# Twelve weight loads of the first expert loop: issued behind the loop's own tile count, one unit at a time

## What is computed

```python
def _L0_ffn_ref(x, gate_w, W1, b1, W2, b2, sW1, sb1, sW2, sb2):
    logits = x_flat @ gate_w.T                       # 8 experts
    probs = softmax(logits)
    top_w, sel = top_k(probs, 2)                     # two experts for each token
    top_w = top_w / sum(top_w)
    h = gelu(einsum('th,ehf->tef', x_flat, W1) + b1) # H = 256, F = 1024
    y = einsum('tef,efh->teh', h, W2) + b2
    out = einsum('teh,te->th', y, combine)
    out = out + gelu(x_flat @ sW1 + sb1) @ sW2 + sb2 # one shared expert
x = x + tanh(g_xattn[0]) * L0_xattn(layernorm(x), ctx)
x = x + tanh(g_ffn[0])   * L0_ffn(layernorm(x))
x = x + tanh(g_xattn[1]) * L1_xattn(ctx, layernorm(x))
x = x + tanh(g_ffn[1])   * L1_ffn(layernorm(x))
```

## Time and profile before

| what | us |
|---|---|
| median of 3 runs | 801.63 |
| lowest and highest | 799.29, 803.27 |
| the profiled execution | 800.92 |
| its span in the trace | 799.1 |
| PE busy | 686.3 (86%) |
| DVE busy | 512.9 (64%) |
| ACT busy | 462.8 (58%) |
| POOL busy | 311.2 (39%) |
| mean granted TensorE clock | 0.915 of 2.4 GHz |

### The profile page before, as it was taken

One profiled execution on the slowest core, in us unless ns is written; L12 is line 12 of the kernel. 1 busy time (PEld: TensorE's weight loads), 2 busy tenths in 40 slices (PEclk: granted clock), 3 DMA queues, 4 the chain that ended last, 5 costly groups with the idle time before them and its releaser, 6 DMA issues.

```text
span 799.1 us, 22223 instructions
## 1 busy us (share of the span) xinstructions
PE 686.3 (86%) x7654; PEld 604.3 (76%) x7655; DVE 512.9 (64%) x1286; ACT 462.8 (58%) x1124; POOL 311.2 (39%) x227
## 2 busy tenths in 40 slices
PE   4787899988958999999999918771799999999993
PEld 3454566767858999999989917661689999999993
DVE  4569758796855975777755445948398555555551
ACT  2346668856527976777755605440497656556561
POOL 1100124335541554555544422340256545455442
PEclk9878889999988999999999977955799999999997
DMA  8950100013429433688753359528223232232331
GB/s 264 296 185 27 53 1 1 35 46 130 136 81 369 81 52 65 140 242 228 221 164 49 38 151 408 206 97 228 65 47 48 47 51 46 46 53 42 49 47 21
DMA packets 63235, 91.07 MB, mean 114 GB/s; under 512 B 6203, under 2 KB 48965, under 8 KB 62422
## 3 DMA queue, kind: packets, MB, share of 16 engines
q1 hardware_dynamic: 48118, 69.69, 25.9%
q0 software_dynamic: 15072, 20.84, 16.6%
HBM read 63.73 MB, written 26.79 MB: 113 GB/s over the span
## 4 chain that ended last, share of the span: by engine, by line
PE 63%; DVE 15%; DMA 9%; issue 5%; ACT 5%; SPq 1%; POOL 1%; POOLq 0%; DVEq 0%; ACTq 0%
PE bank L1123 8%; PE bank L1125 7%; PE bank L1124 7%; PE bank L1136 6%; PE bank L1137 6%; PE bank L1138 6%; DMA x_arena<-token_rows,gather_now 4%; PE bank L1106 2%; DMA x_sum<-x_arena,add_now 2%; DMA out<-x_arena,add_now 2%; DVE weights L1568 2%; DVE ln_stats L1890 2%; PE bank L849 2%; PE bank L1019 1%; PE bank L1021 1%
## 5 line engine op out<-in xcount | busy, mean ns | idle before, releaser
L1419 ACT ACTIVATE work<-bank,b_cols 128x128 f32<-128x128 f32 x624 | 177.5, 371 | 172.1 <-PE bank L1125 154.8
L1123 PE MATMUL bank<-x_arena,weights 128*128 128x128 f16 x1248 | 220.2, 222 | 0.3 <-DVE x_arena L1801 0.3
L1124 PE MATMUL bank<-x_arena,weights 128*128 128x128 f16 x1248 | 220.1, 221 | 0.0
L1125 PE MATMUL bank<-x_arena,weights 128*128 128x128 f16 x1248 | 219.8, 221 | 0.0
L1816 DVE TENSOR_TENSOR work<-work 128x512 f16<-128x512 f32 x156 | 101.2, 690 | 140.6 <-ACT work L1427 118.4
L1137 PE MATMUL bank<-weights,work 128*128 x624 | 170.1, 273 | 0.0
L1136 PE MATMUL bank<-weights,work 128*128 x624 | 170.1, 273 | 0.0
L1138 PE MATMUL bank<-weights,work 128*128 x624 | 170.1, 273 | 0.0
L715 POOL DMA_INDIRECT x_arena<-token_rows,gather_now x80 | 100.2, 1252 | 78.3 <-issue 53.8
L1124 PEld LDWEIGHTS bank<-x_arena,weights 128*128 x1248 | 124.2, 100 | 0.0
L1123 PEld LDWEIGHTS bank<-x_arena,weights 128*128 x1248 | 122.8, 98 | 1.1 <-issue 0.5
(11 more groups left out here) (219 smaller groups left out, 1263.5 us busy)
## 6 DMA issues: line engine op xcount, KB each, us to landing
weights<-in_L_ffn_W SPq DMA_DIRECT2D x76, 256.0 KB, 7.7
raw<-in_L_ffn_W SPq DMA_DIRECT2D x44, 256.0 KB
split_dram<-row_arena SPq DMA_DIRECT2D x12, 512.0 KB
weights<-split_dram SPq DMA_DIRECT2D x3, 2048.0 KB, 15.4
token_rows<-row_arena SPq DMA_DIRECT2D x2, 2072.0 KB, 11.3
x_arena<-in_x SPq DMA_DIRECT2D x4, 512.0 KB, 6.6
weights<-in_L_ffn_sW SPq DMA_DIRECT2D x8, 256.0 KB, 7.3
x_sum<-x_arena SPq DMA_DIRECT2D x4, 512.0 KB, 2.9
```

The costliest lines, as they stand in the source:

```text
L1123: nc.tensor.matmul(o, w1_at[f][c][0].block(), hi, start=c == 0, stop=False)
L1124: nc.tensor.matmul(o, w1_at[f][c][0].block(), lo, start=False, stop=False)
L1125: m = nc.tensor.matmul(o, w1_at[f][c][1].block(), hi, start=False, stop=c == DC - 1)
L1419: m = nc.scalar.activation(hid[:, k, f * P:f * P + P], h_ps[k][half][:, g * P:g * P + P], ACT.Gelu, bias=b1_cols[n][:, f, bass.ds(e, 1)], ...
```

## The change

SP's three waits ahead of the units 24 to 35 (the routing, the stored rows, the end of the shared expert) become one wait for the end of the shared expert, and ahead of each unit stands a wait for `rowT_done[0]`, the number of tiles that PE has turned. The count wanted is 2 + (u - 24) * 2 // 3: 2, 2, 3, 4, 4, 5, 6, 6, 7, 8, 8, 9 for u = 24 to 35. Count c is reached when `turn(c - 1)` is done, at the head of body c - 2.

```diff
             biases(0)
-            sp.wait_ge(routed, 1)
-            for u in range(24, 28):
-                load_unit(0, u)
-            sp.wait_ge(rows_stored[0], 16)
-            for u in range(28, 32):
-                load_unit(0, u)
             sp.wait_ge(s_down_done, STEPS)
-            for u in range(32, 36):
+            for u in range(24, 36):
+                sp.wait_ge(rowT_done[0], 2 + (u - 24) * 2 // 3)
                 load_unit(0, u)
```

## The result

The forecast was 799.6 us, a little faster. The changed kernel took 806.4 us (median of 20 runs, 801.3 to 809.0) against 802.08 (20 runs, 799.2 to 806.4) in the same session: ratio 1.0046, interval 1.003 to 1.0062. It is slower by 0.46%, and its median lies outside the range of 797.0 to 802.8. The two intervals do not meet, so the size of the loss is not the same from session to session; what both exclude is the gain of 2.0 us that was forecast, a ratio of 0.9975.

What follows compares the result with a forecast made beforehand. PE was taken to bound the settled loop, with slow gathers in the load burst delaying its start. Gains of 2.1 (turn 5) and 0.27 (tile 6) less 0.35 (collisions) gave 2.0 us: median 799.6 us, range 797.0 to 802.8.

Steps and rivals of the forecast that it cites:

- The first stall: At tile 2: PE's 2.21 us stall for its gather goes, the gather taking about 4.5 us instead of 7.47.
- ACT is next: At tile 1's gelus: ACT's split of units 20 and 21 holds them until 248.0, leaving 1.0 us of gain.
- The second gather: At tile 5: gather 5 takes 3.60 to 4.63 us, and turn 5 moves from 264.63 to about 262.5, 2.1 us.
- the rival with more than one gain: From turn 2 on: gather 5 lands before PE needs it, turn 5 at 261.2, 3.5 us, 798.1; chance 0.17.
- The clock: Body from 245.96 to 253.14, 7.18 us at low clock: full clock gives nothing more, covered by gather 5.
- Tile 6 and after: From turn 6 on: up to 0.27 us gained, against 0.35 us lost once to loads colliding with gathers.
- The late gathers: Gathers of tiles 6 to 9 meet weights and take 7.47 us; turn 7 2.0 us late, 803.6; chance 0.08.
- The stretch at 340 us as a witness: At 340 to 360 us: one load and store per tile, PE busy 20.00 of 20.00 us, supporting a low collision cost.
- Edits at no cost: On SP: new waits block only SP; the first two layer-1 units behind them are covered by 30 us.
- The rule of the Trainium skill: DMA engines alternate between queues by packet, so a gather in the burst is slowed by no more than its own length.
- A late unit: At ACT's splits: units 30 and 31 come late, at most 0.7 us at the worst row; chance 0.03.

Runs made afterwards that it cites:

- e13: The kernel of e7 with all sixteen splits of late units moved two bodies on; 0.9963 (0.9948 to 0.9979) against the kernel before.
- e9: The changed kernel itself again, in a second session, against the kernel before; 1.0007 (0.9989 to 1.0026).
- e12: The changed kernel again, nothing edited, for a third trace; turn 8 at 49.3 us and turn 20 at 117.5 us after the issue of gather 0.
- e6: Changed kernel with units 24 to 35 not loaded, splits reading other data, first two layer-1 units loaded after the last split; 0.9960 (0.9938 to 0.9982).
- e7: Changed kernel, but units 24 to 31 in one wave after turn 1, then one per body after up matmuls, first two layer-1 units last; 0.9989.
- e16: Changed kernel with the twelve waits moved behind the up matmuls and the first two layer-1 units waiting for tiles 10 and 11; 0.9999.
- e15: The kernel of e7 run again against the kernel before; 0.9977 (0.9957 to 0.9997).
- e1: Changed kernel, but all twelve late units go out in one burst once tile 1 is turned; 1.001 (0.9988 to 1.0033).
- e4: Changed kernel, but units 24 to 29 at once after turn 1, then one unit per body after its up matmuls; 1.0013 (0.9985 to 1.0042).
- e5: Changed kernel, with the first two layer-1 units also waiting for tiles 10 and 11; 1.0004 (0.9982 to 1.0027).
- e10: The kernel of e5 again, beside the changed kernel on one chip; 0.9995 (0.9978 to 1.0012).

## Why the prediction was wrong, point by point

- **The first stall**: right. Turn 2 waits 0.27 us, and not for its gather, where it had waited 2.21, and stands 1.9 us ahead (forecast 2.2). Gather 2 left the burst.
- **ACT is next**: right to within 0.2 us. The gelus of tile 1 were forecast at 248.0, which with the 3.52 us of the later start is 251.5; the line below has 251.44. Gather 5 was forecast at 258.3, so 261.8; POOL issues it at 261.95. Timeline of ACT, tile 1:

```profile
251.44 2.19 ACT L1414 ACTIVATE work<-bank,b_cols 128x128 f32<-128x128 f32 x8
```

- **The second gather**: turn 5 gained 1.6 us, forecast 2.1. Within the bounds of the term. A time beside it was wrong: at full clock PE is at turn 5 not by 261.2 but by 260.4, three bodies of 5.54 us after 243.75 (e13 took 16.6 us for the three). The forecast did not hang on it; the rival with more than one gain would have been 4.2 us, not 3.5.
- **The clock**: this term failed too. It was put down as covered. That was true for the clock gained after turn 2, but the same price came back elsewhere: behind the wait of 2.19 us at turn 8 the clock fell, and the step from turn 8 to 9 took 7.82 us, 0.56 of them a wait. Windows of the changed kernel (length, busy us of PE, PEld, DVE, ACT, POOL, clock, DMA share, GB/s):

```profile
284.00:286.00 2.00, 1.25 (x12) 0.88 (x9) 1.42 (x4) 1.89 (x3) 0.00 (x0) 1.00 0.87 247
286.00:288.00 2.00, 0.56 (x6) 0.56 (x7) 1.90 (x4) 0.00 (x0) 0.47 (x1) 0.83 0.07 26
288.00:290.00 2.00, 2.00 (x22) 2.00 (x20) 0.83 (x4) 0.00 (x0) 1.70 (x2) 0.50 0.37 124
290.00:292.00 2.00, 2.00 (x31) 2.00 (x30) 0.00 (x0) 1.14 (x4) 0.41 (x1) 0.82 1.01 220
```

  PE works without a pause from 288 on, but at 1.2 GHz until about 291. That is 1.7 us for one wait, on top of it.
- **Tile 6 and after**: this is the step that failed. It priced a collision at 0.35 us, once, because a late PE gives the gathers their slack back. Turns 4, 5, 6, 8 and 9 of the changed kernel wait 0.94, 0.90, 1.24, 2.19 and 0.56 us, 5.8 in all, 1.8 of it by turn 5; with the slow clock the lead of 1.6 us at turn 5 became a loss of 4.8 at turn 9. In e9 and e12 turn 20 is 4.0 and 1.8 us behind the mean of the kernel before. The slack did not come back because only gathers had been counted. The adds were left out, though the earlier trace rows had one that waited 3.48 us for the add before it. Adds that land after 6.2 to 7.4 us, where those of e6 took 3.7 to 5.1, hold the next add, and that the next gather, so the delay is passed on from tile to tile. The late gathers were a rival, at a chance of 0.08 and a price of 2.0 us, by gathers of 7.47 us. It came in part: gathers 8 and 9 took 5.9 and 5.8 us from issue to turn, the sign that had been named, but they were also issued late, behind the adds, and of that the rival had nothing.
- **The stretch at 340 us as a witness**: it did not carry over. There SP issues its load when a split is done, not when a tile is turned, and only one for each tile. What was taken from it was the rate of bytes. In e7, too, single loads behind the up matmuls, one in a body, left turns 6 to 20 without a wait.
- **Edits at no cost**: wrong. The layer-1 pair was looked at only for its deadline, 30 us later. That it would leave SP together with unit 35, as 1.5 MB beside one gather and one add, was not asked. It cost 0.7 to 4.2 us in the three traces of the changed kernel, 1.6 more than without it by the estimate above, out of 3.5 us by which these traces are behind at turn 20.
- **The rule of the Trainium skill** ("DMA: Bandwidth & Descriptors", section "Queues, rings and completion order"), turns packet by packet: the gather beside a single load took 5.8 us against 3.9 without one (e16, e6), 1.9 more. By the prediction's reading of the rule it would be no more than its own 0.74, which takes the packets of both sides to be equally long; no run here tests that. As at the earlier trace rows, the trace has more delay than that reading allows.
- **A late unit**: right that it is no matter. No split waited.

## What to carry to other kernels

When transfers are spread out to keep them off the first waits, list everything else that uses the DMA engines in the stretch they are moved to, with what each is chained to: a transfer that waits for its predecessor (here the accumulating add) passes every delay on. Ask also what is queued behind the last moved instruction, since a wait in a row of DMAs bunches up all that follow it. And when a stall goes, look for the next bound from the start of the stretch, not from the stall: here it was four splits in bodies 0 and 1. Moving those on top of the one wave (e13) gave 0.9963, where the wave alone (e7, e15) had given 0.9989 and 0.9977. And a trace is one execution: set its time beside the median of its own kernel before its microseconds are added up.

## What the runs showed of the hardware

- A wait of PE can cost nearly twice its length. Ahead of turn 2 or a later one it waited 2.05 to 2.85 us ten times in these traces. Behind nine of these waits the granted clock went to half, and the body took 6.99 to 8.39 us in place of 5.54 (in the changed kernel 0.56 us of its 7.82 are a new wait). It stayed full behind the tenth (2.30 us, e1), behind one of 3.10 us (e16) and behind all that were 1.61 us or less. What tells the cases apart stays open.
- An accumulating DMA of 128 rows of 1 KB landed after 3.7 to 5.1 us with no load in flight (e6). With loads issued around it, it took up to 7.4 us in the changed kernel (279.22, above), 7.7 in e4 and, right behind the burst, 9.1 in e1; but also 4.2, beside a single unit (274.12).
- The same code, up to turn 8, put that turn between 47.0 and 51.5 us in five traces (changed, e9, e12, e5, e10). Where POOL's and SP's transfers are issued within a few tenths of each other, one trace does not give the size of an effect.
